# A token mixer's square-root iteration in 64x64 products on single images, with a vector column and gates per group of eight images

## The reference

```python
# y = layer norm of x over the 64 channels (no affine, eps 1e-6)
xs = y.reshape(b, c, M)                  # c = 64 rows of M = 256 numbers
cov = xs @ I_hat @ xs.T                  # I_hat centres each row and divides by M
A = cov / trace(cov)
ZY = 0.5 * (3I - A);  Y = A @ ZY;  Z = ZY
for _ in range(1, 4):
    ZY = 0.5 * (3I - Z @ Y);  Y = Y @ ZY;  Z = ZY @ Z
ZY = 0.5 * Y @ (3I - Z @ Y)
v = mean over the last axis of ZY * sqrt(trace(cov))     # 64 numbers per image
gate = sigmoid(W2 @ relu(W1 @ v + b1) + b2)              # centre taps of two 3x3 convs
x = x + gate * y
```

## Time and profile before

| | us |
|---|---|
| median of 3 runs | 381.18 (378.8 to 381.83) |
| the profiled execution | 379.0 |
| its span, first to last instruction | 377.2 |
| PE busy / weight loads | 307.6 / 203.4 |
| DVE, ACT, POOL busy | 246.5, 157.5, 150.6 |
| mean granted clock of TensorE, share of full | 0.905 |

### The profile page before, as it was taken

One profiled execution on the slowest core, in us unless ns is written; L12 is line 12 of the kernel. 1 busy time (PEld: TensorE's weight loads), 2 busy tenths in 40 slices (PEclk: granted clock), 3 DMA queues, 4 the chain that ended last, 5 costly groups with the idle time before them and its releaser, 6 DMA issues.

```text
span 377.2 us, 8730 instructions
## 1 busy us (share of the span) xinstructions
PE 307.6 (82%) x3441; PEld 203.4 (54%) x3441; DVE 246.5 (65%) x701; ACT 157.5 (42%) x293; POOL 150.6 (40%) x156
## 2 busy tenths in 40 slices
PE   0077789995564989889878899997879999999995
PEld 0066779885532766557655565664534444544442
DVE  6968634559697677787756969966243564655653
ACT  1056242331124555655536444555242545445441
POOL 7976205315439777622001228998208200000000
PEclk9998768987565899999989999999677999999999
DMA  7330000000007777866688100000000000000001
GB/s 228 73 88 12 3 1 0 2 2 0 1 2 179 175 167 167 224 164 169 162 195 199 27 2 3 3 2 3 0 0 2 10 20 30 30 30 30 30 2 56
DMA packets 16740, 23.45 MB, mean 62 GB/s; under 512 B 7892, under 2 KB 12540, under 8 KB 16700
## 3 DMA queue, kind: packets, MB, share of 16 engines
q1 hardware_dynamic: 16700, 22.90, 24.0%
HBM read 20.54 MB, written 2.36 MB: 61 GB/s over the span
## 4 chain that ended last, share of the span: by engine, by line
PE 43%; DMA 15%; POOL 15%; DVE 11%; issue 10%; ACT 4%; SPq 1%; POOLq 0%; DVEq 0%; ACTq 0%
DMA c_dram<-cT 8%; PE pair L1701 8%; PE pair L1714 8%; PE pair L1689 7%; DMA hid<-c_dram 5%; PE pair L1600 4%; POOL ln_rstd L594 3%; PE pair L1389 3%; POOL rstd L473 3%; DMA xs_ffn<-c_dram 2%; PE pair L1379 2%; PE pair L1358 2%; POOL rstd L540 1%; PE pair L1726 1%; ACT sqj L1129 1%
## 5 line engine op out<-in xcount | busy, mean ns | idle before, releaser
L1084 DVE SCALAR_TENSOR_TENSOR hid<-pair,neg_shift,YZ 128x512 f32<-128x512 f32 x64 | 45.1, 747 | 40.4 <-PE pair L1701 40.4
L1310 ACT ACTIVATE hid<-pair,bn 128x1024 f32<-128x1024 f32 x32 | 38.6, 1205 | 43.6 <-PE pair L1689 43.5
L1226 ACT ACTIVATE pair<-pair,cols 128x512 f32<-128x512 f32 x64 | 39.6, 657 | 34.8 <-PE pair L1526 34.7
L594 POOL TENSOR_TENSOR ln_rstd<-ln_var,neg_half 128x8 f32<-128x8 f32 x16 | 26.4, 1657 | 49.6 <-DVE ln_var L835 49.6
L1526 PE MATMUL pair<-xs,w1f 64*64 64x256 f32 x512 | 37.0, 408 | 2.2 <-DVE scaled L813 2.0
L1553 PE MATMUL pair<-scaled,w 64*64 64x256 f32 x512 | 35.6, 382 | 0.0
L1701 PE MATMUL pair<-hid,f 64*64 64x512 f32 x256 | 34.9, 617 | 0.0
L1714 PE MATMUL pair<-hid,fo 64*64 64x256 f32 x512 | 34.3, 384 | 0.6 <-DVE hid L1084 0.6
L1689 PE MATMUL pair<-xs_ffn,f1f 64*64 64x512 f32 x256 | 34.2, 606 | 0.0
L1600 PE MATMUL pair<-xp,vconv 64*64 64x256 f32 x512 | 32.4, 400 | 0.0
L1714 PEld LDWEIGHTS pair<-hid,fo 64*64 64x64 f32 x512 | 18.9, 136 | 20.7 <-issue 14.9
(11 more groups left out here) (218 smaller groups left out, 589.1 us busy)
## 6 DMA issues: line engine op xcount, KB each, us to landing
xs_ffn<-c_dram SPq DMA_DIRECT2D x32, 256.0 KB, 5.3
hid<-c_dram SPq DMA_DIRECT2D x32, 256.0 KB, 5.6
out_dram<-x SPq DMA_DIRECT2D x8, 256.0 KB, 2.4
x<-in_x_dram SPq DMA_DIRECT2D x3, 512.0 KB, 6.6
x<-in_x_dram SPq DMA_DIRECT2D x2, 256.0 KB, 3.1
w1f<-in_L_ffn_w_dram SPq DMA_DIRECT2D x2, 128.0 KB
w<-in_L_ffn_w_dram SPq DMA_DIRECT2D x2, 128.0 KB
f1f<-in_L_ffn_W_dram SPq DMA_DIRECT2D x2, 128.0 KB
```

Of the source, the lines that this page charges most:

```text
L594: g.tensor_tensor(ln_rstd[:, st, b % 2, :], ln_var[:, st, b % 2, :], neg_half[:, 0:T2], ALU.pow).then_inc(ln_rstd_ready[st], 1)
L1084: v.scalar_tensor_tensor(out=hid2[:, n % 2, u, :].rearrange("p (j n) -> p j n", j=2), in0=h, scalar=neg_shift2[:, k, u:u + 1], in1=w, op0= ...
L1226: s.activation(h, h, ACT.Gelu, bias=cols[:, e:e + 1]).then_inc(hidden_gelu, 1)
L1310: s.activation(hid1[:, n % 2, :, :], pair_of("layer1", n)[:, :, :], ACT.Relu, scale=bn1[:, 0, k:k + 1], bias=bn1[:, 1, k:k + 1]).then_inc( ...
```

## The change

It rewrites the first stage.

- Token norm: the standard deviation comes from ACT (`Sqrt` of var/4, a table function) and one correction step on DVE (reciprocal, multiply, add, reciprocal), in place of POOL's power. ACT then writes 10 of a group's 16 token slots as `x * rstd + bias` in single 64-wide instructions, POOL the other 6 in two instructions. DVE's subtract, multiply and row sum go, and so does the centring: a row holds whole tokens that were each centred.
- The trace comes from the token variances (`share`) by one small product and a reduction on DVE; `Square` on ACT goes.
- The iteration keeps one matrix per image, `Pm` (from A), with a 65th column that carries the vector of ones through it. A half step `square` multiplies `Pm` by itself, DVE takes `Qm = Pm - t * Pm Pm`; a half step `cube` multiplies `Pm` by `Qm`, DVE takes the new `Pm`. All products use 64x64 weights of one image, image j on partitions 64j to 64j+63, and write partitions 64j up of **the same bank**. There are 4 squares and 3 cubes per group, then two products with one column (`third`, `fourth`). ACT's copies and DVE's diagonal copies go, and so do `Zd`, `Td` and POOL's two memsets of them.
- Gate, ReLU and tanh run per group of 4 pairs, the two images of a pair on their own partitions.
- Order: PE transposes the vectors of weights (`vec_rows`) before any other work, so it waits for those 20 small DMAs first; SP issues the two gate weights after them, now four DMAs, and `w1f`, `w2` and `b2m` after `wd`, `wc` and the gate weights. DVE's copies `b2sel` and `neg_shift2` move from ahead of block 0 to ahead of `route(0)`.

```diff
@@ products
-            def prod_p(n):
...
-                    last = t.matmul(bank[gr % 2][:, C * i:C * (i + 1)], Zd[:, k, :], YZ[:, k, 0, :], start=True, stop=True)
...
-                    last = t.matmul(bank[2 + gr % 2][:, P * i:P * (i + 1)], Td[:, k, :],
-                                    YZ[:, k, :, :].rearrange("p s c -> p (s c)"), start=True, stop=True)
...
+            def square(gr, k):
...
+                n = C if k == 2 else C + 1
                 for i in range(GP):
+                    for j in range(2):
+                        last = t.matmul(state(gr, n)[halves(j), i, :], Pm[halves(j), GP * gr + i, 0:C], Pm[halves(j), GP * gr + i, 0:n],
+                                        start=True, stop=True)
+                last.then_inc(ns_square[gr], 1)
...
+            def gram(gr):
...
+                pe.wait_ge(rows_T_copied, 2 * gr + 2)
+                pe.wait_ge(trace_ready, gr + 1)
...
+                            img = xT[:, gr % 2, c, P * i + C * j:P * i + C * (j + 1)]
+                            last = t.matmul(state(gr, C)[halves(j), i, :], img, img, start=(c == 0), stop=(c == 1))
@@ PE's queue, start
+            pe.wait_ge(w_vec, W_VEC)
+            t.transpose(bank[7][:, 0:NROWS], vec_rows[:, :], ident[0:NROWS, 0:NROWS]).then_inc(vecs_ready, 1)
+            traces(0)
             rows_out(0)
+            traces(1)
             gram(0)
...
@@ vector
+            def take_q(gr, k):
...
+                v.scalar_tensor_tensor(out=Qm[:, group(gr), 0:n], in0=state(gr, n), scalar=-THIRD[k], in1=Pm[:, group(gr), 0:n],
+                                       op0=ALU.mult, op1=ALU.add).then_inc(ns_q[gr], 1)
@@ vector's queue, end of the stage
+            take_q(2, 3)
+            take_q(3, 3)
+            apply_third(2)
+            apply_third(3)
+            apply_fourth(2)
+            apply_fourth(3)
+            moe_mult(0)
+            gate_rows(2)
+            gate_rows(3)
+            moe_stats(1)
+            moe_sub(1)
+            moe_mult(1)
@@ scalar
+            def half_std_of(gr):
...
+                s.activation(half_std[:, gr % 2, :], quarter_var[:, gr % 2, :], ACT.Sqrt).then_inc(tok_half_std, 1)
+            def tok_norm(gr):
...
+                for t in range(SCALAR_SLOTS):
+                    last = s.activation(ng[:, t, :], xg[:, t, :], ACT.Identity, scale=tok_rstd[:, gr % 2, t:t + 1],
+                                        bias=tok_bias[:, gr % 2, t:t + 1])
```

More of the change, by code:

```diff
@@ new lines, in _ @@
+            tok_aggr(3)
+            traces(1)
+            take_p(0, 0)
+            normal(1)
+            tok_chain(3)
+            take_q(0, 1)
+            take_q(1, 0)
+            take_p(0, 1)
+            take_p(1, 0)
+            take_q(0, 2)
+            take_q(1, 1)
+            traces(2)
+            take_p(0, 2)
+            take_p(1, 1)
+            normal(2)
+            take_q(0, 3)
+            take_q(1, 2)
+            apply_third(0)
+            take_p(1, 2)
+            apply_fourth(0)
@@ new lines, in _ @@
+            take_q(1, 3)
+            traces(3)
+            apply_third(1)
+            normal(3)
+            apply_fourth(1)
+            gate_rows(0)
+            take_q(2, 0)
+            gate_rows(1)
+            take_q(3, 0)
+            take_p(2, 0)
+            x1_gated(0)
+            take_p(3, 0)
+            take_q(2, 1)
+            x1_added(0)
+            take_q(3, 1)
+            take_p(2, 1)
+            take_p(3, 1)
+            scale_f2()
+            moe_stats(0)
+            take_q(2, 2)
@@ new lines, in fourth, with gate_conv1 @@
+            def fourth(gr):
+                pe.wait_ge(third_applied, gr + 1)
+                for i in range(GP):
+                    for j in range(2):
+                        last = t.matmul(bank[gr][halves(j), COL_FOURTH + i:COL_FOURTH + i + 1], Qm[halves(j), GP * gr + i, 0:C],
+                                        cvec[halves(j), GP * gr + i:GP * gr + i + 1], start=True, stop=True)
+                last.then_inc(fourth_vec, 1)
+            def gate_conv1(gr):
+                pe.wait_ge(y_ready, gr + 1)
+                pe.wait_ge(w_gate, W_GATE)
+                for j in range(2):
+                    last = t.matmul(bank[gr][halves(j), COL_C1:COL_C1 + GP], gw1[halves(j), :], yv[halves(j), group(gr)], start=True, stop=True)
+                last.then_inc(conv1_done, 1)
@@ new lines, in gate_conv2, with gate_spread @@
+            def gate_conv2(gr):
+                pe.wait_ge(conv1_relu, gr + 1)
+                for j in range(2):
+                    last = t.matmul(bank[gr][halves(j), COL_C2:COL_C2 + GP], gw2[halves(j), :], g1[halves(j), group(gr)], start=True, stop=True)
+                last.then_inc(conv2_done, 1)
+            def gate_spread(gr):
+                pe.wait_ge(gate_rows_ready, gr + 1)
+                wait(pe, gate_ready, gr - 1)
+                pe.wait_ge(rows_T_copied, 2 * NG)
+                t.matmul(bank[4 + gr % 2][:, 0:GP * C], same_img[:, :], gspread[:, group(gr), :].rearrange("p i c -> p (i c)"),
@@ L1491, in _ @@
             last.then_inc(conv_v, 1)
-            z_times_u(1)
-            y_times_zu(1)
+            square(2, 1)
+            square(3, 1)
+            pe.wait_ge(bn_step, 10)
+            for k in range(KP):
+                last = t.transpose(bank[6][:, P * k:P * (k + 1)], rep(bn2[:, 0, k:k + 1], 1, P), ident[:, :])
+            last.then_inc(s2_spread, 1)
+            cube(2, 1)
+            cube(3, 1)
+            square(2, 2)
+            square(3, 2)
+            cube(2, 2)
+            cube(3, 2)
+            square(2, 3)
+            square(3, 3)
+            third(2)
+            third(3)
+            fourth(2)
+            fourth(3)
             def moe_x(b):
```

776 lines of the change are left out of this document (329 added, 447 removed).

## The result

The changed kernel takes 358.12 us (median of 4 runs, 354.83 to 359.6), the kernel before 381.5 in the same session: ratio 0.938, 95% interval 0.928 to 0.947. Forecast were 350.5, range 338 to 366. The profiled run took 359.34 (span 357.6, granted clock 0.900); before it was 379.0 and 0.905. So by the profiles 19.6 us were gained, and 28.4 were expected.

A forecast was written before the change was run, and what follows sets the result against it. The chain to block 0's weight copy (POOL's power, DVE, slowly clocked PE) was taken to bound the first stage; four steps summed to 76.3 us at 2.4 GHz, 99.1 at 1.2, taken as 84: 379.0 - 28.4, rounded to 350.5, range 338 to 366.

The forecast's parts named there:

- The likeliest case: Stage up to block 0's weight copy: tiles side by side, clock between the levels, 343 to 359 us, chance 0.62.
- the pure 2.4 GHz case: Stage up to block 0's weight copy at 2.4 GHz, with 3 us for meetings beside POOL unspent: 338 us, the range's lower end.
- The half step: Iteration on PE: 16 instructions on two corners side by side, 0.55 us at 2.4 GHz, 0.93 at 1.2.
- Step 1: From the start to the first Gram done: 17.8 us, before 26.1, with the vector rows landing at 12.2.
- Step 2: From first to last Gram: 24.4 us with 2.4 GHz from 25 us on, 35.7 at 1.2 throughout, before 32.8.
- Step 3: From the last Gram to the last gate vector: 16.4 us at 2.4 GHz, 26.5 at 1.2, before 39.3.
- Step 4: From last gate vector to block 0's weight copy: 14.7 or 16.1 us by clock, plus 3 for meetings; before 14.2.
- 1 (clock 1.2 throughout): Rival: the clock stays at 1.2 GHz up to block 0's weight copy, 365.7 us; chance 0.12.
- 2 (corners in sequence): Rival: the two corners run one behind the other, 1.09 us a half step, 362.3 us; chance 0.18.
- 3: Rival: corners one behind the other and the clock at 1.2 GHz besides, slower at 405.9 us; chance 0.04.
- 4: Rival: the gain stops at block 0's weight copy because the experts' start hangs on something else, 379 us; chance 0.04.
- a gain ahead of the copy passes whole into the time: Behind block 0's weight copy the program is unchanged, so the 28.4 us gained ahead of it come off 379.0.

The follow-up runs named there:

- the delayed one: Changed kernel with 16 unused products of 256 columns in VectorE's queue right ahead of route(0), 5.5 us of delay: 366.87 us, ratio 0.967.
- The order's run: Changed kernel with all products of the upper corner first, then all of the lower corner's, in half steps and Grams: 368.81 us, ratio 0.978.
- set A: Changed kernel with 64x64 by 65-column products added behind its end, here on the two diagonal corners in turn, one bank: 31 ns an instruction.
- C: Same run of the changed kernel with products added behind its end, here on the upper corner alone: 55 ns an instruction.
- best1: Changed kernel with traces early, f2 and block 0's statistics spread behind takes, block 1's statistics earlier, small copies in the mixing loop: 347.72 us, ratio 0.902.
- best2: best1 with route(0) ahead of block 1's multiply, and block 0's weights ahead of block 1's columns on TensorE and ScalarE: 344.74 us, ratio 0.901.

## Why the prediction was right, and where it was off

**The sum of the front.** The likeliest case came: tiles side by side, a clock between the levels. That the tiles run side by side in one bank was reasoned from rows with a bank each, and held. The third of the way at 1.2 GHz was a choice between two bounds, with no mechanism that gives it; by the granted clock in 20 to 70 us the five profiles named next had between 32% and 46%. Its sum was 84, the copy came at 87.6. By steps, with a third at 1.2 GHz, it was 17.8 + 28.2 + 19.8 + 18.2, and the misses are 0.7, 0.8, 2.5 and -0.4. The unedited orders gave 87.6 and 88.7, the delayed one 92.7 - 5.46 = 87.2, the one with late copies 84.9 + 3.4 = 88.3, and the one with the corners measured behind the end 90.5 (granted clock 0.68 and 0.64 in 40 to 60 us, 0.85 and 0.81 in the first): that is how far the copy moves with the same instructions in front of it. The range's lower end has a slip: the pure 2.4 GHz case with the 3 us unspent gives 379.0 - (112.4 - 73.3) = 339.9, not 338.

**The half step** was priced at 0.55 and 0.93; it shows 0.68 and 1.13; a single such instruction at 2.4 GHz is shown with 0.22 from start to end (in the run with the corners alone), and that much lies behind the last start. Between starts it is 16 x 31 ns = 0.50 us, which the walk had as 0.47. At the higher clock a half round of two groups takes 1.21 us on TensorE (58.95 to 60.16), less than the 1.5 assumed.

**Step 1** was right within 0.7: the vector rows landed at 13.2, not 12.2.

**Step 2** took 29.0; a third of the way at 1.2 GHz the forecast's bounds give 24.4 + 11.3 / 3 = 28.2. The waits for traces (3.7) were not in it: where `traces(1)`, `traces(2)` and `traces(3)` stand in VectorE's queue was not priced at all, and the run with them ahead shows that it was worth 3.2 us by the end of this step. That the miss is only 0.8 means that other terms were too high, the half rounds among them; so the step came near by errors on both sides.

**ACT's slots** were priced 0.16 to 0.27, from activations of 4 to 16 columns; with 64 columns and scale and bias read from memory they are 0.34. The prediction named this as a way to be wrong. No run shows that it cost time: with six slots the ratio is 0.942, with ten 0.938.

**Step 3** is the largest miss of the front, 22.3 against 16.4 + 10.1 / 3 = 19.8. Spreads and convolution weights were put at 3 us; from start to start they take 1.15, 0.63, 1.93 and 0.58 = 4.3 us, while TensorE is busy without a gap from 50 to 60. That is 1.3 of the 2.5; the rest is not traced. The 2.37 us ahead of `take_q(2, 2)` were in the sum (2.4). The table load shows as 0.39 of waiting on VectorE, where 0.2 was said: 1.28 us lie between 49.05 and 50.35, and nothing else. The Trainium skill (ScalarE: Activation LUTs, What ACT_TABLE_LOAD costs) counts another drain of 1.38 us; the trace does not agree.

**Step 4** was right, 17.8 against 18.2 (17.7 at 2.4 GHz, 19.1 at 1.2), with luck: the small copies took 3.4 and not 1.8, which ate 1.6 of the 3 us set aside for meetings beside POOL, and the one meeting that was foreseen took 1.1 (1.74 for 0.69).

**Rivals.** 1 (clock 1.2 throughout) did not come. 2 (corners in sequence) is refuted by the run that measures them alone: 31 ns against 55. By the rule of the Trainium skill (TensorEngine Tiling (Array Packing), Restrictions and Gotchas), that different row tiles cannot access one bank simultaneously, set A should have gone at the pace of C; the measurement decides, and it went at the pace of two banks, each corner writing its own half of the partitions. The order's run shows what such a sequence would have cost even in part: 10 us of time. 3 falls with it. 4 falls with the result itself, 358 and not 379, and with the delay.

**The step that failed** is "a gain ahead of the copy passes whole into the time". It took the part behind as a fixed length, and that part took 270 us in the changed kernel's profiles and 265 in those of before. The table shows that it takes 264.2 to 270.3 with the very same instructions behind the copy (leaving out the late copies, `best1` and `best2`), split into 102.6 to 106.0 for the experts and 82.1 to 85.8 for the stretch behind them. The clock is in it: from the copy on, the changed kernel's two profiles have 41 us at 1.2 GHz, those of before 30.7 and 23.8. For the second stretch this accounts for the loss (2.2 of the 5.1 us); for the experts it fits, but other profiles took as long with less. The changed kernel had 0.67 and 0.56 in 250 to 270 us; the one with six slots on ACT, whose experts end within 1 us of the same moment (193.8 and 193.1), had these stretches and took 3.6 us less:

```profile
250.00:260.00 10.00, 7.54 (x51) 3.90 (x49) 4.10 (x12) 5.26 (x8) 0.00 (x0) 0.92 0.01 2
260.00:270.00 10.00, 9.17 (x84) 4.35 (x88) 4.03 (x7) 2.53 (x3) 7.32 (x6) 0.83 0.01 2
```

So of the 7.6 us by which the time is over the forecast, 3.6 come from the front and 5.1 from behind the copy, less 1.2, by which the profiled run lies over its median; the last 0.1 is rounding. Why the five profiles with the changed kernel's front all have a long part behind (267.8 to 270.3, where it can be told) and those with another order in front mostly not stays open: it could be where the clock's changes fall after such a front, or chance.

**What is not shown.** Of the 23 us gained, the runs test the alternation of corners (10 us) and the place of the roots (6 by the medians). What one matrix per image, the vector column and the copies left out are worth by themselves no run shows.

## What to carry to other kernels

Small products cost here by the number of instructions and by how many corners of the array neighbours in the queue use: put 64x64 products on alternating corners before shortening anything else. When two engines hand over to each other in written order, look for the step that needs little but stands behind much in its queue (here three reductions of 16 columns); taking away a wait earlier in the same queue showed no gain while that one stayed. Move small work off the path only to a place with real slack, and don't credit a gain in front to the last microsecond: here the part behind it varied by 6 us in 360 with the same instructions, and a forecast of a median should start from medians, not from one profiled execution.

## What the runs showed of the hardware

- 64x64 weights with 65 columns in f32, at 2.4 GHz: 55 ns an instruction on one corner, 29 to 31 on two (diagonal or of the same rows, one bank or two), 16 on four.
- The same instructions in the same order ran at a granted clock of 0.68 (twice), 0.75, 0.85 and 1.00 in 40 to 50 us, in different executions, and in `best1` at 0.50 for 20 us while TensorE was always busy: how busy it is in a stretch does not tell its clock.
- The stretch from the experts' last add to the feed-forward layer took 82.1 us with 10 us of it at 1.2 GHz and 85.8 with 20.5, with the same instructions.
- Four copies of 64x4 on VectorE took 2.65 us beside POOL, 0.66 each, where four of the same took 1.04 in the kernel before. That row is not quite undisturbed: POOL was at work for the first 0.67 us of it too. With the copies late they took 2.06, with POOL at work nearly throughout.
